# Node stage of a two-layer graph network moved into the chunk loop of the first layer

## The reference

```python
# layer 0
h = x @ Wx.T + bx
A = W_ac - W_ac.T - 0.1 * eye(128)
q, k, v = h @ Wq.T + bq, h @ Wk.T + bk, h @ Wv.T + bv
e = concat([edge_attr, cos(abs(node_vec[src] - edge_weight)[:, None] * time_w + time_b)]) @ We.T
alpha = sum(q[dst] * (k[src] + e)) / sqrt(128)          # then a softmax over the edges of each dst
m = segment_sum((v[src] + e) * softmax(alpha), dst)
h = h + tanh(h @ A.T + m + b_ac)
x1 = layernorm(x + tanh(h))
# layer 1
edge_new = relu(concat([x1[src], x1[dst]]) @ We1 + be1) @ We2 + be2
agg = segment_sum(edge_new, dst)
mesh_new = relu(concat([x1, agg]) @ Wn1 + bn1) @ Wn2 + bn2
out = layernorm(2 * x1 + mesh_new)
```

## Time and profile before

| what | value |
|---|---|
| time, median of 3 runs | 5171.55 us (5166.94 to 5185.83) |
| span of the profiled execution, first to last instruction | 4156.7 us |
| busy: PE, DVE, ACT, POOL | 75%, 59%, 42%, 73% of the span |
| mean granted TensorE clock | 0.822 of full speed |
| layer 0, first to last gather issued | 53.3 to 2011.2 us |
| layer 1, first to last gather issued | 2175.2 to 4125.2 us |

### The profile page before, as it was taken

One profiled execution on the slowest core, in us unless ns is written; L12 is line 12 of the kernel. 1 busy time (PEld: TensorE's weight loads), 2 busy tenths in 40 slices (PEclk: granted clock), 3 DMA queues, 4 the chain that ended last, 5 costly groups with the idle time before them and its releaser, 6 DMA issues. The chain is left out here.

```text
span 4156.7 us, 73778 instructions
## 1 busy us (share of the span) xinstructions
PE 3100.8 (75%) x18778; PEld 2820.4 (68%) x18779; DVE 2472.7 (59%) x5456; ACT 1733.9 (42%) x2900; POOL 3014.0 (73%) x3193
## 2 busy tenths in 40 slices
PE   6888887888888888888666666666667677766675
PEld 4777777777777777777546666666666666666665
DVE  4877777777777777777574444444444444454544
ACT  3767776777777777777461111111111111111111
POOL 5777777777777777777347777777777777777775
PEclk8999999999999999999896666666666666767677
DMA  6333333333333333333233333333333333333332
GB/s 187 81 81 83 81 83 81 83 81 82 82 81 82 81 82 82 81 82 82 75 102 101 89 92 89 92 89 91 91 89 93 91 96 93 94 95 94 94 95 61
DMA packets 419860, 370.13 MB, mean 89 GB/s; under 512 B 269651, under 2 KB 347883, under 8 KB 419724
## 3 DMA queue, kind: packets, MB, share of 16 engines
q0 software_dynamic: 100032, 217.87, 20.5%
q1 hardware_dynamic: 308544, 143.31, 13.5%
q10 hardware_dynamic: 11214, 8.17, 0.7%
HBM read 347.56 MB, written 21.44 MB: 89 GB/s over the span
## 5 line engine op out<-in xcount | busy, mean ns | idle before, releaser
L721 POOL DMA_INDIRECT he<-h_table,src_i x1563 | 1477.5, 945 | 515.7 <-issue 505.3
L1642 POOL DMA_INDIRECT msg<-p_table,src x1563 | 1474.8, 944 | 484.1 <-issue 484.1
L1659 PE MATMUL p_edge<-r_win,hotT 80*128 80x128 f32 x3136 | 656.7, 395 | 589.2 <-DVE msg L1780 575.2
L1659 PEld LDWEIGHTS p_edge<-r_win,hotT 80*128 80x128 f32 x3136 | 606.6, 297 | 630.5 <-issue 536.8
L1715 ACT ACTIVATE msg<-msg 128x1024 f32<-128x1024 f32 x196 | 207.2, 1057 | 1649.0 <-DVE msg L1780 1649.0
L1780 DVE TENSOR_TENSOR msg<-msg,p_edge 128x512 f32<-128x512 f32 x392 | 251.9, 684 | 979.1 <-DMA msg<-p_table,src 979.1
L1670 PE MATMUL p_sumT<-msg,hot 128*80 128x129 f32 x3136 | 601.0, 372 | 34.4 <-ACT sumT L1723 34.4
L1670 PEld LDWEIGHTS p_sumT<-msg,hot 128*80 128x80 f32 x3136 | 580.0, 224 | 51.3 <-issue 51.2
L760 PE MATMUL p_score<-qk_two,heT 128*128 128x160 f32 x1568 | 394.9, 335 | 166.2 <-ACT heT L870 164.4
L762 PE MATMUL p_score<-qk_win,heT 128*128 128x80 f32 x3136 | 462.7, 272 | 0.0
L762 PEld LDWEIGHTS p_score<-qk_win,heT 128*128 128x128 f32 x3136 | 451.9, 199 | 0.0
(11 more groups left out here) (205 smaller groups left out, 4114.8 us busy)
## 6 DMA issues: line engine op xcount, KB each, us to landing
dst_row<-in_dst_dram SPq DMA_DIRECT2D x196, 320.0 KB
feat<-in_edge_attr_dram SPq DMA_DIRECT2D x196, 128.0 KB
he<-h_table,src_i POOLq DMA_INDIRECT x1563
msg<-p_table,src POOLq DMA_INDIRECT x1563
qk_win<-qk_table SPq DMA_DIRECT2D x196, 40.0 KB
qk_two<-qk_table SPq DMA_DIRECT2D x392, 20.0 KB
r_win<-r_table SPq DMA_DIRECT2D x196, 40.0 KB
qk_table<-qk SPq DMA_DIRECT2D x13, 512.0 KB
```

Source lines behind the costliest of these rows:

```text
L721: e.indirect_dma_start(out=he[u][:, j, 2 * FE:2 * FE + ROW], out_offset=None, in_=h_table[:, :], in_offset=bass.IndirectOffsetOnAxis(ap=sr ...
L1642: e.indirect_dma_start(out=msg[u][:, j, 0:D], out_offset=None, in_=p_table[:, :], in_offset=bass.IndirectOffsetOnAxis(ap=src_i[u][:, j:j + ...
L1659: mm = e.matmul(p_edge[h][:, j % 4, :], hotT_of(c)[:, j, :], r_win[u][:, :], start=True, stop=True)
```

## The change

The node stage block is gone. Its work is done in layer 0's loop: from turn 15 on, in each of 13 turns, a group of four blocks whose edges are all done goes through the stage, spread over the turn's seven chunk steps (u = c[1]). Two groups (13 and 14) are left for the end of the loop, where they follow one another. The work is now by rows (nodes on partitions), so 1/den is a column beside each row and needs no DRAM, and x needs no transposes. It uses the PSUM banks of the turns (p_turn[0..2]); so PE's turn(c+2) waits in steps 1, 5 and 6 until the node work has read them. hT is stored to DRAM once and its SBUF becomes the buffers of the node work; h by rows, h turned and x are loaded by SP in each turn. x1 turned is stored to DRAM (x1T_dram) and loaded again in layer 1, a group per turn, where 2 * x1 is now added by four more matmuls of PE with a doubled identity (twice). Weights of layer 1 are loaded and multiplied at the start of layer 1, where DVE also clears acc.

```diff
+            def node_take(e, n, b, k):
...
+                e.activation(node_acc, acc[:, 0, bass.ds(at, G)], ACT.Copy)
+                e.activation(node_m[k][0:A2, :, :], by_block(acc[0:A2, 1, bass.ds(at, G)]), ACT.Copy).then_inc(acc_taken, 1)
+
+            def node_values(e, n, k):
...
+                for j in range(GB):
+                    here = slice(j * D, (j + 1) * D)
+                    e.matmul(p_turn[2][:, j:j + 1], second[:, j, :], ident[0:A2, A2 - 1:A2], start=True, stop=True)
+                    e.matmul(p_turn[1][:, here], second[:, j, :], we_bvT[:, :], start=True, stop=False)
+                    e.matmul(p_turn[1][:, here], first[:, here], wvT[:, :], start=False, stop=True)
+                    e.matmul(p_turn[0][:, here], node_hT[k][:, here], aT[:, :], start=True, stop=False)
+                    mm = e.matmul(p_turn[0][:, here], ones[0:1, :], bac_r, start=False, stop=True)
+                mm.then_inc(val_full, 1)
+
+            def node_anti(e, n, k):
...
+                e.activation(node_m[k], by_block(p_turn[0][:, :]), ACT.Copy).then_inc(anti_done, 1)
+
+            def node_pre(e, n, k):
...
+                e.tensor_scalar(node_den[k], p_turn[2][:, 0:GB], 1.0e-16, None, ALU.add).then_inc(den_done, 1)
+                e.wait_ge(den_done, n1)
+                e.reciprocal(node_rden[k], node_den[k]).then_inc(rden_done, 1)
+                e.wait_ge(rden_done, n1)
+                e.wait_ge(anti_done, n1)
+                for j in range(GB):
+                    here = slice(j * D, (j + 1) * D)
+                    op = e.scalar_tensor_tensor(out=node_m[k][:, j, :], in0=p_turn[1][:, here], scalar=node_rden[k][:, j:j + 1],
+                                                in1=node_m[k][:, j, :], op0=ALU.mult, op1=ALU.add)
+                op.then_inc(pre_done, 1)
...
+                e.activation(node_m[k], node_m[k], ACT.Tanh).then_inc(upd_done, 1)
...
+                e.tensor_tensor(node_m[k], node_m[k], node_h[k], ALU.add).then_inc(h2_done, 1)
...
+                e.activation(node_m[k], node_m[k], ACT.Tanh).then_inc(tanh_done, 1)
...
+                e.tensor_tensor(node_m[k], node_m[k], node_x[k], ALU.add).then_inc(y_done, 1)
...
+                    op = e.bn_stats(node_stats[k][:, j, :], node_m[k][:, j, :])
...
+                    op = e.bn_aggr(node_mv[k][:, j, :], node_stats[k][:, j, :])
...
+                e.activation(node_std[k], node_mv[k][:, :, 1:2].rearrange("p b o -> p (b o)"), ACT.Sqrt, bias=eps_c[:, 0:1]).then_inc(root_done, 1)
...
+                e.reciprocal(node_rstd[k], node_std[k]).then_inc(rstd_done, 1)
...
+                    op = e.tensor_scalar(node_m[k][:, j, :], node_m[k][:, j, :], node_mv[k][:, j, 0:1], node_rstd[k][:, j:j + 1], ALU.subtract, ALU.mult)
...
+                    mm = e.transpose(p_turn[1][:, j * P:(j + 1) * P], node_m[k][:, j, :], ident[:, :])
...
+                e.activation(x1T_g, p_turn[1][:, :], ACT.Copy).then_inc(x1T_done, 1)
...
+                for q in range(2):
+                    for j in range(GB):
+                        mm = e.matmul(p_turn[q][:, j * D:(j + 1) * D], x1T_g[:, j * P:(j + 1) * P], we1[:, q, :], start=True, stop=True)
...
+                e.activation(p_rows, by_block(p_turn[0][:, :]), ACT.Copy).then_inc(p_done, 1)
...
+                e.tensor_tensor(r_rows, by_block(p_turn[1][:, :]), be1_b.unsqueeze(1).broadcast_to([P, GB, D]), ALU.add).then_inc(r_done, 1)
...
+                e.dma_start(x1T_dram[:, bass.ds(at, G)], x1T_g).then_inc(x1T_out, 16)
...
+                e.dma_start(p_table[bass.ds(at, G), :].rearrange("(b p) d -> p b d", p=P), p_rows).then_inc(p_out, 16)
...
+                e.dma_start(r_table[bass.ds(at, G), :].rearrange("(b p) d -> p b d", p=P), r_rows).then_inc(r_out, 16)
...
+                            e.dma_start(hT_dram[:, :], hT[:, :]).then_inc(hT_out, 16)
...
+                        def step_grouped(c, k):
+                            u = c[1]
+                            if u == 1:
+                                step(c, lambda: node_values(e, k, 0), lambda: e.wait_ge(pre_done, val(e, k + 1)))
+                            elif u == 5:
+                                step(c, lambda: node_turn(e, k, 0), lambda: e.wait_ge(x1T_done, val(e, k + 1)))
+                            elif u == 6:
+                                def tables_read():
+                                    e.wait_ge(p_done, val(e, k + 1))
+                                    e.wait_ge(r_done, val(e, k + 2))
+
+                                step(c, lambda: node_tables(e, k), tables_read)
...
+                        def step_grouped(c, k):
+                            u = c[1]
+                            if u == 2:
+                                step(c, lambda: node_update(e, k, 0))
+                            elif u == 3:
+                                step(c, lambda: node_tanh(e, k, 0))
+                            elif u == 4:
+                                step(c, lambda: node_root(e, k, 0))
+                            elif u == 5:
+                                step(c, lambda: node_copy_x1(e, k))
+                            elif u == 6:
+                                step(c, lambda: node_copy_p(e, k))
...
+                                node_take(e, k, pick_block(e, k), 0)
+                            elif u == 1:
+                                node_anti(e, k, 0)
+                            elif u == 6:
+                                node_store(e, k, pick_block(e, k))
+                                node_store_r(e, k, pick_block(e, k))
...
+                        def step_grouped(c, k):
+                            u = c[1]
+                            step(c)
+                            if u == 1:
+                                node_pre(e, k, 0)
+                            elif u == 2:
+                                node_h2(e, k, 0)
+                            elif u == 3:
+                                node_moments(e, k, 0, 0)
+                            elif u == 4:
+                                node_normal(e, k, 0)
+                            elif u == 6:
+                                node_copy_r(e, k)
...
+                            e.memset(acc[:, 0, :], 0.0)
+                            e.memset(acc[0:1, 1, :], 0.0)
...
-                    mm = e.matmul(p_mesh[:, k * D:(k + 1) * D], hid[:, k * P:(k + 1) * P], wn2[:, :], start=True, stop=True)
+                    e.matmul(to, hid[:, j * P:(j + 1) * P], wn2[:, :], start=True, stop=False)
+                    mm = e.matmul(to, x1_g[k][:, j * P:(j + 1) * P], twice[:, :], start=False, stop=True)
```

More of the change, by code:

```diff
@@ L224, in gnn_kernel @@
             FIRST = 16 * 5
[L225 removed]
+            LOADS = 16 * 10
             @block.sync
@@ L695, in _ @@
                                 load_src((0, u))
+                            chunks(e, load, apart_first=load_apart)
                         else:
@@ L825, in _ @@
                         turn((0, 1))
-                        chunks(e, step)
+                        if at_first:
+                            e.sem_inc(x1_full, 1)
+                            chunks(e, step, grouped=step_grouped, ahead=1)
+                        else:
+                            chunks(e, step)
                         spread_top((TURNS - 1, SLOTS - 1))
@@ L1085, in _ @@
                         masks((0, 0))
-                        chunks(e, step)
+                        if at_first:
+                            e.sem_inc(r_done, 1)
+                            e.sem_inc(r_out, 1)
+                            chunks(e, step, grouped=step_grouped, ahead=1)
+                        else:
+                            chunks(e, step)
                         add((TURNS - 1, SLOTS - 4), starts[3])
@@ L1477, in gnn_kernel @@
             fixed = sem("fixed1")
+            loads = sem("loads1")
+            x1_in = sem("x1_in")
+            w_full = sem("w_full1")
+            w_done = sem("w_done1")
+            LOADS1 = 16 * 6
             out_done = sem("out_done1")
```

603 lines of the change are left out of this document (329 added, 274 removed).

## The result

The changed kernel took 5269.4 us, median of 4 runs (5259.21 to 5274.03), beside 5169.24 us, median of 4 (5152.51 to 5185.83), for the kernel before: a ratio of 1.0192 (1.0162 to 1.0221), slower by 100 us where 54 us faster were forecast. Its profiled execution took 5274.03 us, 1.8 us more than its span.

The account below looks back on a forecast made before the run. POOL's issue of gathers was taken to bound both loops, with 163.1 us standing still between them. Terms -70.7 + 11 + 3.5 + 2.1 = -54 us on 5171.6 gave 5117 us, range 5095 to 5170.

Parts of the forecast that it names:

- The 1014.9 us: Timed median 5171.55 us above the profile's span of 4156.7: not shown in the trace, left unchanged by the change.
- a sign of its being wrong: Wrong would be a turn over 75 us, a tail over 130, or another share of the 1015 us outside the span.
- POOL's issue of gathers sets the pace of both loops: Both layers' loops: gathers 1.253 us apart, so 10.0 us per chunk and 70 us per turn.
- 13.4 us of room a turn: Layer 0's loop: free steps take 8.09 us each, 56.6 of a 70 us turn, leaving 13.4 for node work.
- 11 us lost: Layer 0's loop: 0.85 us a turn over 13 turns, the middle of nothing and 1.7 over the room; 0 to 22.
- slower: Rival, layer 0's loop: work lies in series, 8.4 us a turn over the 70, 5215 us; break-even 5.0; chance 0.13.
- PE's values: node_values, 16 large and 4 one-column matmuls per group: 4.9 us at full clock, 8.8 at half.
- 70.7 us gained: Between the layers: the 163.1 us without gathers shrink to 92.4, with two serial groups in them.
- the drain: End of layer 0: last sums 33.8 us after the last gather before, 39.4 with group 13's values and acc copies.
- 3.5, 2.1 and nothing: Last turn's delay in the drain 3.5 us lost, doubled mesh product ending layer 1 2.1 lost, other parts nothing.
- Transfers at nothing: Layer 0's new loads delay nothing queued behind; x1 loads in layer 1 and the hT store cost nothing.
- The gathers held up by DVE: Rival: DVE's SBUF-to-SBUF work stops POOL 2.8 us a group, 36 us more, 5153 us; chance 0.05.

Follow-up runs that it names:

- e1: The kernel before, run and profiled once more unchanged: 5164.74 us, span 5162.1.
- exceptional execution: The kernel before, unchanged, in the profile that the prediction was made from: span 4156.7 us.
- e2: Changed kernel without the 13 groups in layer 0's turns, three whole-table stores at its start instead: 5130.86 us, ratio 0.9917.
- e12: Changed kernel with four gathers in a chunk in place of eight: 3538.67 us, ratio 0.6858 against the full kernel before.
- e8: Changed kernel with 12 matmuls instead of 20 in node_values in 12 of the 13 turns: 5277.32 us, ratio 1.0121.
- e7: Changed kernel without the groups' PE, ACT and DVE work in layer 0's turns, their loads, stores and semaphores kept: 5160.31 us, ratio 0.9897.
- e5: Kernel before with four gathers for a chunk instead of eight, both layers, all turns but the first: 3412.61 us, ratio 0.6545.
- e14: Kernel before with two of a chunk's eight plain loads left out in layer 0, all turns but the first: 5136.64 us, ratio 0.9934.
- e11: Kernel before with gathers of half-width rows (288 bytes) in layer 0, all turns but the first: 5208.54 us, ratio 0.9995.
- e13: Kernel before with gathers of 64 rows in place of 128 in layer 0, all turns but the first: 5218.44 us, ratio 1.0113.
- e9: Kernel before with each chunk's eight gathers cut into two bursts of four, a wait between: 5454.7 us, ratio 1.0473.
- e4: Kernel before without eight lines of unneeded semaphore increments on ACT in layer 0: 5174.91 us, ratio 0.9987.
- e6: Kernel before with 60 more semaphore increments on SyncE per chunk of layer 0, from the second turn on: 5908.91 us, ratio 1.1332.
- e3: Changed kernel with node_values moved behind the sums of its step instead of ahead of them: 5294.03 us, ratio 1.0229.

## Why the prediction was wrong, step by step

- **The 1014.9 us** ("I leave them as they are") are the step that failed first. They are no time outside the span, but 2.9 us a chunk in layer 0 and 2.0 in layer 1 (e1): 589 and 385 of the 1005 us between the two spans. The prediction named this as a sign of its being wrong, and the profile before could have shown it: an execution 20% below the median of the runs isn't the one that the median measures.
- **"POOL's issue of gathers sets the pace of both loops"** holds for the exceptional execution only. In the usual one POOL waits for PE's sums and for the stops, and issue is 472 of the 1055 us that it idles.
- **"13.4 us of room a turn"** falls with it. A loop at 12.9 us a chunk has time in it in which engines stand, but DVE, ACT and POOL stand at the same time, and a group's work is added to it (e2, e12), PE's part with the rest (e8).
- **"11 us lost"**, 0.85 a turn, measured 160: 12.9 a turn. The parts together were of the right size: if all of them count, the prediction had 15.1 us a turn, and if the work lies wholly in series 21.8. e12 gives 18.2 where the gathers set no pace at all. What was wrong was taking the room off this, and then the middle of what was left. The rival *slower* had the mechanism, "the work lies in series", and its break-even at 5.0 us a turn was passed by more than twice; even its 8.4 over the pace was too little. Too small among the parts were PE's values: the prediction had 4.9 us, or 8.8 at half clock, and took the 4.9. Their 20 matmuls take 5.9 us at the pace of the two blocks at a granted clock of 1.00, and in the first of the 13 turns (1504.83 to 1515.72) 10.9 without a pause at 0.50.
- **"70.7 us gained"** between the layers measured 57.1. Groups 13 and 14 were near (17.4 for 16.7, 27.6 for 24.4), and 14.9 follow them for 11.9. Mis-sized was the drain: 57.4 to the last sums, not 39.4 and the 3.5 of the last turn's delay. Part of this is the exceptional execution again: in e1 the drain takes 40.7 us without the change, not 33.8. Group 12's normalizing, transposes, tables and three DMA issues and group 13's values (6.8 us on PE, 4.9 forecast) stand in the rest. The whole stretch is 175.3 us in e1, not 164, which gives 11 back.
- **3.5, 2.1 and nothing** for the rest: the drain holds the first; the end of the kernel grew by 3.1, the start by 1.5, layer 1 by 2.2. Transfers at nothing is right (e7).
- **The gathers held up by DVE** are not seen. POOL's gathers by window, plain turns and then turns with a group (count, busy, mean ns, idle):

```profile
L966 POOL DMA_INDIRECT he<-h_table,src_i x623 | 608.5, 977 | 392.4 <-remote 187.7 <-issue 174.3 <-PE p_sum L1031 30.4
...
L966 POOL DMA_INDIRECT he<-h_table,src_i x512 | 491.1, 959 | 447.1 <-PE p_sum L1031 205.3 <-issue 143.5 <-remote 98.3
```

A gather takes 959 ns beside a group and 977 without one, and the idle time ahead of it that ends with PE's sums grows from 30 to 205 us. The longer gathers that the prediction drew from the rule of the Trainium skill (SBUF — State Buffer, section "SBUF: two separate sides") don't show in this row. The rule itself isn't tested by it: it speaks of DVE in a two-port mode, and no run here shows whether the added instructions ran in one.

The measured terms add up to 160.4 - 57.1 + 3.1 + 2.2 + 1.5 = 110.1, the difference of the spans, as they must, since the five stretches make up a span. These are single executions; the medians lie 100 us apart.

Open is what holds PE's releases in a stop. It goes with the number of gather instructions (e5), hardly with plain loads (e14), and not with their bytes, rows or spacing (e11, e13, e9) or ACT's marks (e4). But the exceptional execution issued the same eight gathers a chunk without a stop, so their number alone doesn't make one, and whether it is their number or the time that POOL spends on them no run tells apart. That the recording of the execution is part of it was not ruled out: e6, meant for that, ran into another bound. On such a mechanism the Trainium skill, NOTIFIC — the notification-queue block, section "7.1 Overflow: three behaviours, one of which stalls the engine", says that the internal pipeline of the block that writes the records always holds back its producers rather than lose a record; no run here shows that this is what happens.

## What to carry to other kernels

Before room is read from a profile, its span is to be held against the timed median; where they lie 20% apart, the profile shows another execution, and one more profile of the unchanged kernel costs less than a wrong forecast. Work that is moved into a loop is free only where the loop has time that nobody waits for: here the slack had been read from an execution that the median doesn't measure, and each turn paid for its group, wherever in the step PE's values stood (e3). The two prices should be set beside each other first: a group cost 12.9 us in the loop and its leaving saved 57.1 / 13 = 4.4 between the layers.

## What the runs showed of the hardware

- With four of the eight indirect DMAs a chunk took 4.2 us less (12.9 to 8.7), while half of their bytes (13.02) or half of their rows (13.11) made no difference. The exceptional execution took 10.0 with all eight. The gather of 64 rows took 899 ns, that of 128 rows 947.
- In layer 0 the granted clock was 0.80 where PE stood in the stops (e1), 0.98 nearly without them (e5), and 0.90 in e12's turns with a group. In the same kernel five matmuls of node_values, each with its own weights, took 1.44 to 1.51 us at 1.00 and 2.73 at 0.50.
